# Gate computed transposed for tile pairs, output projection per head pair with the row sums applied in its addition, rotary steps divided anew

## What is computed

```python
H, KV, D = (16, 4, 128)                 # 16 query heads in 4 groups that share k and v
qkv = x @ w_qkv.T                       # q, gate, k, v
q = _layernorm(q, q_norm_w, q_norm_b)   # over the 128 channels of a head
k = _layernorm(k, k_norm_w, k_norm_b)
q = _rope(q, cos, sin); k = _rope(k, cos, sin)
scores = q @ k.T / sqrt(D)              # causal
attn = softmax(scores)
out = (attn @ v) * sigmoid(gate)
attn_out = out @ w_o.T
y = x + attn_out + top2_of_8_experts(xn)   # relu(xn @ w_fc)**2 @ w_proj, weighted
```

## Time and profile before

| | us |
|---|---|
| time, median of 3 runs (1535.32 to 1535.76) | 1535.37 |
| the profiled execution's own time | 1536.22 |
| its span, first to last instruction | 1534.4 |
| PE busy | 1501.5 |
| DVE busy | 1304.1 |
| ACT busy | 1152.4 |
| POOL busy | 364.7 |

### The profile page before, as it was taken

One profiled execution on the slowest core, in us unless ns is written; L12 is line 12 of the kernel. 1 busy time (PEld: TensorE's weight loads), 2 busy tenths in 40 slices (PEclk: granted clock), 3 DMA queues, 4 the chain that ended last, 5 costly groups with the idle time before them and its releaser, 6 DMA issues.

```text
span 1534.4 us, 29715 instructions
## 1 busy us (share of the span) xinstructions
PE 1501.5 (98%) x10589; PEld 1380.6 (90%) x10589; DVE 1304.1 (85%) x3037; ACT 1152.4 (75%) x3017; POOL 364.7 (24%) x502
## 2 busy tenths in 40 slices
PE   5999999999999999999999999999999999999998
PEld 3889999999989999999998999999999899999998
DVE  8999888888998888788799888877879888887788
ACT  4777776778887778777878777777787877768765
POOL 6545434420322111111042211111104221011010
PEclk8999999999999999999999999999999999999999
DMA  5411011011121111111111110111022211001013
GB/s 175 163 38 46 28 43 51 30 53 49 60 60 49 35 42 49 39 39 39 59 59 59 40 49 12 49 39 39 20 74 63 60 49 42 18 22 31 9 50 124
DMA packets 45124, 78.82 MB, mean 51 GB/s; under 512 B 4784, under 2 KB 30896, under 8 KB 44784
## 3 DMA queue, kind: packets, MB, share of 16 engines
q1 hardware_dynamic: 41232, 66.65, 14.2%
q0 software_dynamic: 3744, 10.26, 1.9%
HBM read 58.25 MB, written 24.72 MB: 54 GB/s over the span
## 4 chain that ended last, share of the span: by engine, by line
PE 86%; DVE 8%; ACT 3%; issue 2%; DMA 1%; POOL 1%; SPq 0%; DVEq 0%; ACTq 0%; POOLq 0%
PE bank L1392 45%; PE o_bank L1392 22%; PE pt_bank L1467 14%; PE bank L1445 2%; PE bank L1488 2%; DVE t_same L1266 1%; DVE pT_lo L1316 1%; ACT probs L1017 1%; DVE bank L1299 1%; DVE t_same L1262 1%; ACT pT_hi L1036 1%; DVE neg_chunk_max L1302 1%; DVE sumsq L1234 1%; DVE t_same L1250 1%; PE bank L1509 1%
## 5 line engine op out<-in xcount | busy, mean ns | idle before, releaser
L1017 ACT ACTIVATE probs<-bank,neg_max 128x512 f32<-128x512 f32 (+3 forms) x640 | 400.0, 635 | 100.8 <-DVE neg_max L1309 61.5
L1316 DVE TENSOR_TENSOR pT_lo<-pt_bank,pT_hi 128x512 fp32r<-128x512 f32 (+1 forms) x576 | 369.5, 655 | 87.4 <-ACT pT_hi L1036 82.9
L1036 ACT ACTIVATE pT_hi<-pt_bank 128x512 fp32r<-128x512 f32 (+1 forms) x576 | 326.7, 579 | 119.7 <-PE o_bank L1392 59.3
L1392 PE MATMUL o_bank<-pT_hi,v_hi 128*128 128x256 f32 x1088 | 331.8, 305 | 0.4 <-DVE pT_lo L1316 0.3
L1467 PE MATMUL pt_bank<-ident_rows,probs 128*128 128x128 f32 x2176 | 313.3, 273 | 2.5 <-DVE pT_lo L1316 1.5
L1392 PE MATMUL o_bank<-pT_hi,v_lo 128*128 128x256 f32 x1088 | 307.2, 282 | 0.0
L1392 PE MATMUL o_bank<-pT_lo,v_hi 128*128 128x256 f32 x1088 | 306.6, 282 | 0.0
L1302 DVE TENSOR_REDUCE neg_chunk_max<-bank 128x1 f32<-128x512 f32 (+1 forms) x384 | 244.8, 651 | 58.7 <-PE bank L1392 58.1
L1467 PEld LDWEIGHTS pt_bank<-ident_rows,probs 128*128 128x128 f32 x2176 | 252.1, 140 | 25.2 <-DVE pT_lo L1316 3.8
L1392 PE MATMUL bank<-kT_hi,qT_hi 128*128 128x512 f32 (+3 forms) x640 | 242.7, 379 | 0.7 <-ACT probs L1017 0.6
L1392 PE MATMUL bank<-kT_hi,qT_lo 128*128 128x512 f32 (+3 forms) x640 | 231.2, 361 | 0.0
(11 more groups left out here) (167 smaller groups left out, 2852.1 us busy)
## 6 DMA issues: line engine op xcount, KB each, us to landing
norm_rows<-kept_tables SPq DMA_DIRECT2D x24, 384.0 KB, 3.1
made_tables<-kept_tables SPq DMA_DIRECT2D x24, 384.0 KB, 3.0
kept_tables<-made_tables SPq DMA_DIRECT2D x16, 384.0 KB, 2.5
rows<-xs SPq DMA_DIRECT2D x23, 258.0 KB, 2.7
expert_raw<-in_w_fc SPq DMA_DIRECT2D x23, 256.0 KB, 3.0
expert_raw<-in_w_proj SPq DMA_DIRECT2D x23, 256.0 KB, 2.7
xs<-in_x_fill SPq DMA_DIRECT2D x11, 516.0 KB, 5.4
w_raw<-in_w_in SPq DMA_DIRECT2D x7, 640.0 KB, 4.2
```

Of the source, the lines that this page charges most:

```text
L1017: act.activation(probs[:, u, h % 2, first:first + width], bank("scores", g, t, h, c)[:, 0:width], ACT.Exp, bias=neg_max[:, u, h % 2:h % 2 ...
L1036: act.activation(pT_hi[:, n % PT_RING, 0:width], pt_bank[n % 2][:, 0:width], ACT.Copy)\
L1316: dve.tensor_tensor(pT_lo[:, n % PT_RING, 0:width], pt_bank[n % 2][:, 0:width], pT_hi[:, n % PT_RING, 0:width].bitcast(F32), ALU.subtract) ...
L1392: ins = pe.matmul(out_ap, s, m, start=(start and done == 1), stop=(stop and done == last))
```

## The change

**Gate.** `G` is now computed transposed, with the gate weights as the stationary operand and 256 tokens (two tiles) as the moving one, for two heads at a time: 24 products of 256 columns for a pair of tiles, where there were 12 of 512. The `GT` transposes and `gate_scale` are gone. `tanh` writes the turned gate, and `og` becomes (gate + 1) times the attention output in one DVE instruction, per head pair.

**Output.** `OUT` is computed per head pair, each head into its own 256 columns. The reciprocal row sum is applied where each head's columns are added to the accumulator: four scalar-tensor-tensor instructions per tile (`out_add`, `out_sum`), where there was one addition. `og_hi` and `og_lo` are per head pair for every tile; before, only for the last.

**Rotary part.** `KV` now stands before `Q`. ACT sums the squares itself, with one accumulating instruction per head (`q_take`, 1002; 994 for k). POOL adds the epsilon and takes the power (`rstd`, 890 and 892); ACT then multiplies q and k with the reciprocal deviation (`qk_norm`, 1012, five instructions), and only then `same` (DVE) and `swap` (POOL) multiply with the tables. In groups 1 to 3 POOL also adds the bias table (880, two instructions), and `rope_b` is one DVE addition; in group 0 DVE adds the bias in two. The PSUM bank of `Q` is freed by `qk_norm` instead of `q_take`.

**Start and the rest.** `X_PARTS` begins with two parts of two tiles; the normalisation of all parts but the first is on ACT (928), with a small DVE instruction for its bias. The second `y_place` of a slot now waits for the first to land. `BEGIN` and `DUE` have other numbers.

```diff
-X_PARTS = ((0, 1), (1, 4), (4, 8), (8, 12), (12, 16))
+X_PARTS = ((0, 2), (2, 4), (4, 8), (8, 12), (12, 16))
...
-FREED_BY = {"Q": "q_take", "KV": "v_lo", "G": "tanh", "QT": "q_lo", "KT": "k_lo", "GT": "og", "OUT": "out_add",
+FREED_BY = {"Q": "qk_norm", "KV": "v_lo", "G": "tanh", "QT": "q_lo", "KT": "k_lo", "OUT": "out_sum",
...
-                    w.wait_ge(qkv_read, 3 * n + 2)
+                    w.wait_ge(qk_normed, n + 1)
+                    w.wait_ge(rotated_done, n)
                     wait_tables(w, g, t)
                     for heads, i in ((slice(0, HG), 0), (slice(HG, HG + 1), 1)):
                         count = heads.stop - heads.start
                         for to, of in ((slice(0, 64), slice(64, 128)), (slice(64, 128), slice(0, 64))):
                             ins = pool.tensor_tensor(t_swap[:, heads, to], qk_raw[:, heads, of],
                                                      rotary(g, t)[:, 1, i:i + 1, to].to_broadcast([P, count, 64]), ALU.mult)
+                    if g == 0:
+                        ins.then_inc(swap_done, 1)
+                        continue
+                    ins.then_inc(swap_parts, 1)
+                    w.wait_ge(swap_parts, n - T + 1)
+                    for heads, i in ((slice(0, HG), 0), (slice(HG, HG + 1), 1)):
+                        ins = pool.tensor_tensor(t_swap[:, heads, :], t_swap[:, heads, :],
+                                                 rotary(g, t)[:, 2, i:i + 1, :].to_broadcast([P, heads.stop - heads.start, D]),
+                                                 ALU.add)
                     ins.then_inc(swap_done, 1)
                 elif kind == "rstd":
                     g, t = a
                     n = g * T + t
+                    w.wait_ge(qkv_read, 3 * n + 3)
+                    w.wait_ge(qk_normed, n)
+                    pool.tensor_scalar(variance[:], sumsq[:, n % 2], D * QK_EPS, None, ALU.add).then_inc(variance_done, 1)
                     w.wait_ge(variance_done, n + 1)
-                    w.wait_ge(rotated_done, n)
                     pool.tensor_tensor(rstd[:], variance[:], minus_half[:], ALU.pow).then_inc(rstd_done, 1)
...
-                    w.wait_ge(y_placed, 32 * m)
+                    w.wait_ge(y_placed, 32 * m + 16 * k)
...
+                elif kind == "norm":
+                    first, last = X_PARTS[a[0]]
+                    w.wait_ge(x_in[a[0]], 16)
+                    w.wait_ge(rstd_x_done, a[0] + 1)
+                    w.wait_ge(bias_x_done, a[0])
+                    for t in range(first, last):
+                        act.activation(xn[:, t, 0:C], acc[:, t, :], ACT.Identity, bias=x_bias[:, t:t + 1], scale=x_rstd[:, t:t + 1])\
+                            .then_inc(xn_done, 1)
...
+                elif kind == "kv_take":
+                    g, t = a
+                    n = g * T + t
+                    w.wait_ge(filled, fill["KV", g, t])
+                    w.wait_ge(same_done, n)
+                    w.wait_ge(swap_done, n)
...
+                    act.activation(qk_raw[:, HG, :], bank("KV", g, t)[:, 0:D], ACT.Copy)
+                    act.activation(bank("KV", g, t)[:, 0:D], bank("KV", g, t)[:, 0:D], ACT.Square,
+                                   accum_out=sumsq[:, t % 2, HG:HG + 1]).then_inc(qkv_read, 1)
+                    act.activation(v_hi[:, t, :], bank("KV", g, t)[:, D:2 * D], ACT.Copy).then_inc(qkv_read, 1)
                 elif kind == "q_take":
                     g, t = a
                     n = g * T + t
                     w.wait_ge(filled, fill["Q", g, t])
-                    w.wait_ge(same_done, n)
-                    w.wait_ge(swap_done, n)
+                    for h in range(HG):
+                        ins = act.activation(qk_raw[:, h, :], bank("Q", g, t)[:, h * D:(h + 1) * D], ACT.Square,
+                                             accum_out=sumsq[:, n % 2, h:h + 1])
+                    ins.then_inc(qkv_read, 1)
+                elif kind == "qk_norm":
+                    g, t = a
+                    n = g * T + t
+                    w.wait_ge(rstd_done, n + 1)
+                    w.wait_ge(qkv_read, 3 * n + 1)
+                    for h in range(HG + 1):
+                        raw = bank("Q", g, t)[:, h * D:(h + 1) * D] if h < HG else qk_raw[:, HG, :]
+                        ins = act.activation(qk_raw[:, h, :], raw, ACT.Identity, scale=rstd[:, h:h + 1])
+                    ins.then_inc(qk_normed, 1)
+                elif kind == "tanh":
+                    g, u, p = a
+                    n = g * T + 2 * u
+                    w.wait_ge(filled, fill["G", g, u, p])
                     if n:
...
+                        w.wait_ge(og_done, 2 * n - 1 + p)
+                    act.activation(gate[:, 2 * p:2 * p + 2, :], bank("G", g, u, p)[:].rearrange("p (h q) -> p h q", h=2),
+                                   ACT.Tanh, scale=0.5).then_inc(gate_done, 1)
...
-                    for h in range(HG):
-                        gh, inv = gate[:, t % 2, h * D:(h + 1) * D], row_inv[:, h:h + 1]
-                        ins = act.activation(gh, gh, ACT.Identity, bias=inv, scale=inv)
-                    ins.then_inc(gated, 1)
...
-                elif kind == "sumsq":
-                    g, t = a
-                    n = g * T + t
-                    w.wait_ge(qkv_read, 3 * n + 2)
-                    dve.tensor_reduce(sumsq[:], squares[:], AX.X, ALU.add).then_inc(sumsq_done, 1)
...
-                    dve.tensor_scalar(variance[:], sumsq[:], 1.0 / D, QK_EPS, ALU.mult, ALU.add)\
-                        .then_inc(variance_done, 1)
...
-                    dve.tensor_tensor(t_same[:], t_same[:], t_swap[:], ALU.add).then_inc(both_done, 1)
-                    w.wait_ge(both_done, n + 1)
-                    w.wait_ge(rstd_done, n + 1)
-                    for h in range(HG + 1):
-                        ins = dve.scalar_tensor_tensor(rotated[:, h, :], t_same[:, h, :], rstd[:, h:h + 1],
-                                                       rotary(g, t)[:, 2, h // HG, :], ALU.mult, ALU.add)
-                    ins.then_inc(rotated_done, 1)
+                    if g:
+                        dve.tensor_tensor(rotated[:], t_same[:], t_swap[:], ALU.add).then_inc(rotated_done, 1)
+                    else:
+                        dve.tensor_tensor(rotated[:], t_same[:], t_swap[:], ALU.add).then_inc(both_done, 1)
+                        w.wait_ge(both_done, n + 1)
+                        dve.tensor_tensor(rotated[:, HG, :], rotated[:, HG, :], table_bias[:, 1, :], ALU.add)
+                        dve.tensor_tensor(rotated[:, 0:HG, :], rotated[:, 0:HG, :],
+                                          table_bias[:, 0:1, :].to_broadcast([P, HG, D]), ALU.add).then_inc(rotated_done, 1)
...
-                    w.wait_ge(gated, i)
-                    dve.reciprocal(row_inv[:], row_sum[:]).then_inc(inv_done, 1)
+                    if i >= 2:
+                        w.wait_ge(acc_done, acc_number["out_sum", *tile_before(g, t, 2), 1])
+                    dve.reciprocal(row_inv[:, t % 2], row_sum[:]).then_inc(inv_done, 1)
                 elif kind == "og":
-                    g, t, p = a if len(a) == 3 else (*a, None)
-                    cols = slice(0, QW) if p is None else slice(256 * p, 256 * p + 256)
-                    w.wait_ge(filled, fill["GT", g, t])
-                    w.wait_ge(o_copied, 2 * (g * T + t) + (2 if p is None else p + 1))
-                    dve.tensor_tensor(oT[:, cols], bank("GT", g, t)[:, cols], oT[:, cols], ALU.mult).then_inc(og_done, 1)
+                    g, t, p = a
+                    n = g * T + t
+                    w.wait_ge(gate_done, g * T + t // 2 * 2 + p + 1)
+                    w.wait_ge(o_copied, 2 * n + p + 1)
+                    o = oT[:, 256 * p:256 * p + 256].rearrange("p (h q) -> p h q", h=2)
+                    dve.scalar_tensor_tensor(o, gate[:, 2 * p:2 * p + 2, t % 2 * P:t % 2 * P + P], 1.0, o, ALU.add, ALU.mult)\
+                        .then_inc(og_done, 1)
...
+                elif kind in ("out_add", "out_sum"):
+                    g, t, p = a
+                    hh = 0 if kind == "out_add" else 1
+                    w.wait_ge(filled, fill["OUT", g, t, p])
+                    w.wait_ge(inv_done, g * T + t + 1)
                     w.wait_ge(acc_done, acc_before[step])
-                    dve.tensor_tensor(acc[:, t, :], bank("OUT", g, t)[:, 0:C], acc[:, t, :], ALU.add)\
+                    dve.scalar_tensor_tensor(acc[:, t, :], bank("OUT", g, t, p)[:, hh * C:(hh + 1) * C],
+                                             row_inv[:, t % 2, 2 * p + hh:2 * p + hh + 1], acc[:, t, :], ALU.mult, ALU.add)\
                         .then_inc(acc_done, 1)
...
-                elif kind == "GT":
-                    g, t = a
-                    w.wait_ge(gated, g * T + t + 1)
-                    for h in range(HG):
-                        ins = pe.transpose(bank("GT", g, t)[:, h * P:(h + 1) * P],
```

(23 more changed lines are left out.)

216 lines of the change are left out of this document (93 added, 123 removed), and 46 rows, old and new, of the table BEGIN.

## The result

The changed kernel takes **1629.7 us** (median of 4 runs, 1624.38 to 1630.55) against 1535.34 before: a ratio of 1.0608, 95% interval 1.0584 to 1.0631. It is 94 us slower; the forecast was 1530, with 1514 to 1543 as its range.

A forecast was written before the change was run, and what follows sets the result against it. PE, busy for 98% of the span, was taken as the bound. PE work -25.0, exposed chain to QT +15, start +2.5, shared bank +2, last tile +0.4 gave -5.1 us: median about 1530, range 1514 to 1543.

The forecast's parts named there:

- the addition: In the chain from Q to QT, POOL's addition of epsilon before the power was put at 0.3 us (0.1 to 1.25).

The follow-up runs named there:

- second experiment: The changed kernel with POOL's sine multiplication and bias addition each replaced by a fill of the same buffer that reads nothing from SBUF; 1588.18 us.
- third experiment: The changed kernel with DVE's cosine multiplication of the four q heads reading q from PSUM, one instruction per head, holding Q's bank until done; 1643.58 us.

## What to carry to other kernels

A busy share of 85% on an engine that works through a fixed order is not 15% of room: before an edit is costed at nothing because PE is full, look for how late its result may be at the next place where PE takes something from that engine, and for what stands behind it in its queue. An order that was made for certain durations must be made again when an operation changes or moves, and judged only then; here that is worth 74 of 94 us, where the kernel before gains 12. Two engines that are released by the same event and read SBUF together should be checked for contention on both sides, with the victim's own queue in view.

The best kernel found is the one before the change in a new order, 1523.1 us.

## What the runs showed of the hardware

A multiplication of 128 columns with both operands in SBUF takes DVE 0.28 us beside a POOL that only writes (second experiment) and 0.71 to 0.78 on average beside one that reads (changed kernel); 512 columns take 0.68 and 1.11. The multiplication with one operand in PSUM was not slowed (341 ns for 128 columns, third experiment). POOL's 64-column pieces lost as well, 0.53 instead of 0.36 us.

POOL's fill of 2560 bytes takes 2.23 us as single bytes, about 0.87 ns for each element. POOL adds a constant to 5 columns in 0.24 us, where the power over the same 5 takes 1.20; the prediction had 0.3 for the addition, with 0.1 to 1.25 as bounds.

The granted clock goes to half, from the level of 2.4 to that of 1.2 GHz, in short stretches after PE has waited, and products of 256 columns then stand 0.21 us apart instead of 0.12. Changed kernel, PE, group 1; PE had waited 1.29 us up to 636.19, and 0.29 just before the first row. The second view gives PE's busy time in the stretch and the granted clock:

```profile
637.58 1.11 PE L1487 MATMUL pt_bank<-ident_rows,probs 128*128 128x128 f32 x4 [0.29 <-DVE pT_lo L1332]
...
638.92 0.41 PE L1412 MATMUL bank<-w_hi,xT_lo 128*128 128x256 f32 x1
639.13 0.41 PE L1412 MATMUL bank<-w_hi,xT_hi 128*128 128x256 f32 x1
```

```profile
637.60:638.70 1.10, 1.10 (x5) 0.50 0.00 0
```

A kernel that makes PE wait a little pays twice. By the mean clock this is some 23 of the 94 us, an estimate that no run isolates.
